# First attention: row tiles in another order, wide rows' softmax sums folded on GpSimd, inverse sums two tiles later

## What is computed

```python
xn = _layernorm(x)
latent_kv = xn @ w_kv_down
k, v = split(latent_kv @ w_kv_up)            # 16 heads x 64
q = xn @ w_q
att = einsum('bqhd,bkhd->bhqk', q, k) * 64 ** -0.5
att = softmax(where(causal, att, -inf))
y = einsum('bhqk,bkhd->bqhd', att, v)
x = x + y @ w_out + ffn(xn)                  # FFN with fp4-rounded inputs and weights
```

## Time and profile before

| | |
|---|---|
| median of 3 runs | 2287.49 us (2284.92 to 2288.25) |
| profiled execution | 2287.97 us |
| its span | 2286.2 us |
| TensorE busy | 2154.7 us, 94% |
| VectorE busy | 1672.4 us, 73% |
| ScalarE busy | 1322.8 us, 58% |
| GpSimd busy | 47.6 us, 2% |
| mean granted TensorE clock | 0.994 |
| one turn, by its first matmul (705.59 to 745.95 us) | 40.36 us |

### The profile page before, as it was taken

How to read it: one execution, slowest core, us unless ns; L and a number is a source line. 1 busy time by engine, 2 the same in 40 slices (tenths; PEclk the granted TensorE clock), 3 DMA queues, 4 the chain that set the end, 5 groups by cost and what they waited for, 6 DMA issues and landing times. The chain is left out here.

```text
span 2286.2 us, 45447 instructions
## 1 busy us (share of the span) xinstructions
PE 2154.7 (94%) x19387; PEld 1343.7 (59%) x19387; DVE 1672.4 (73%) x2210; ACT 1322.8 (58%) x2126; POOL 47.6 (2%) x61
## 2 busy tenths in 40 slices
PE   4999999999999999999999989999999999999998
PEld 2666666676776766767667666544444444444444
DVE  6777777777767777677777775777777777777771
ACT  3655556555565555655556553466666666666666
POOL 5000000000000000000000000100000000000000
PEclk7999999999999999999999999999999999999999
DMA  5000000000000000000000019100001111001000
GB/s 123 1 1 1 1 1 1 1 1 1 1 1 1 1 1 1 1 1 1 1 1 1 1 35 231 48 20 20 20 20 30 27 29 32 20 20 20 11 2 11
DMA packets 41211, 42.60 MB, mean 19 GB/s; under 512 B 21361, under 2 KB 33617, under 8 KB 40882
## 3 DMA queue, kind: packets, MB, share of 16 engines
q1 hardware_dynamic: 39858, 39.05, 7.5%
q10 hardware_dynamic: 1152, 0.64, 0.1%
HBM read 27.71 MB, written 11.70 MB: 17 GB/s over the span
## 5 line engine op out<-in xcount | busy, mean ns | idle before, releaser
L1733 DVE TENSOR_REDUCE nm_half<-slot 128x2 f32<-128x1024 f32 x512 | 606.5, 1222 | 162.8 <-PE slot L1511 118.0
L1714 ACT ACTIVATE pT<-slot 128x1024 f32<-128x1024 f32 x512 | 505.9, 1026 | 270.6 <-PE slot L1620 215.9
L948 ACT ACTIVATE prob<-slot,negmax 128x1024 f32<-128x1024 f32 (+6 forms) x448 | 316.8, 718 | 255.1 <-DVE negmax L1045 181.8
L752 PE MATMUL slot<-k_hl,q_hl 64*128 64x512 f32 (+3 forms) x2560 | 356.1, 359 | 57.7 <-ACT prob L948 54.9
L752 PEld LDWEIGHTS slot<-k_hl,q_hl 64*128 64x128 f32 x2560 | 259.4, 186 | 99.2 <-ACT prob L948 74.3
L790 PEld LDWEIGHTS slot<-ident,prob 128*128 128x128 f32 x2304 | 253.9, 141 | 88.7 <-issue 61.4
L790 PE MATMUL slot<-ident,prob 128*128 128x128 f32 x2304 | 288.6, 275 | 0.9 <-DVE probT L612 0.9
L612 DVE COPY probT<-slot 128x768 f32<-128x768 f32 (+1 forms) x192 | 166.8, 869 | 151.3 <-PE slot L790 148.6
L802 PE MATMUL yspace<-probT,v_sb 128*64 128x512 f32 (+3 forms) x1536 | 276.2, 494 | 0.0
L1586 PE MATMUL yspace<-pT,v 128*32 128x512 f32 x2048 | 266.9, 603 | 1.6 <-ACT y_raw L1701 0.8
L1614 PE MATMUL slot<-qs,ks 49*128 49x512 f32 x1024 | 240.2, 471 | 15.1 <-DVE nm_half L1733 7.5
(11 more groups left out here) (244 smaller groups left out, 2330.3 us busy)
## 6 DMA issues: line engine op xcount, KB each, us to landing
qs<-q_hi SPq DMA_DIRECT2D x64, 64.0 KB
qs<-q_lo SPq DMA_DIRECT2D x64, 64.0 KB
ks<-k_hi SPq DMA_DIRECT2D x64, 64.0 KB
ks<-k_lo SPq DMA_DIRECT2D x64, 64.0 KB
x_tok<-in_L_attn_x_dram SPq DMA_DIRECT2D x4, 512.0 KB, 6.6
q_hi<-qk_out SPq DMA_DIRECT2D x4, 512.0 KB, 4.4
q_lo<-qk_out SPq DMA_DIRECT2D x4, 512.0 KB, 5.3
k_hi<-qk_out SPq DMA_DIRECT2D x4, 512.0 KB, 6.1
```

The costliest lines, as they stand in the source:

```text
L752: nc.tensor.matmul(own_ps[a][:, o:o + m], q_hl[hq][own, i * P:(i + 1) * P], k_hl[hk][own, o:o + m], start=(k == 0), stop=(k == 3 and o + m ...
L948: last = nc.scalar.activation(prob[a][:, p_at(i, 0, w)], ps[:, o:o + w], ACT.Exp, bias=negmax[:, i, a:a + 1], accum_out=sums[:, i, a:a + 1])
L1714: nc.scalar.activation(pT[hp][m % PT_DEEP][:, :, :], slot[at["x", n] % RING][:, :].rearrange("p (j t) -> p j t", t=BANK), ACT.Exp)\
L1733: nc.vector.tensor_reduce(nm_half[:, h, :, p * TPB + i], slot[pos % RING][:, :].rearrange("p (a t) -> p a t", t=BANK), AX.X, ALU.max, nega ...
```

## The change

- `s_list` has the two heads of tile 4 first, then 7, 6, 3 and 5. The items in `yspace` are now (7, 1) and (5, 1). `LONE` is gone: both slots of a pair of items are claimed ahead of its first pass.
- The exponentials of the nine wide items no longer accumulate. GpSimd sums instead: `row_sums(it)` takes both heads of a tile at once, adds the right half of the row to the left half, and does this four times (`FOLDS`), so that 1/16 of the width is left in `parts`. These are 20 additions a turn, each waiting for the one before it. Tiles 0 to 2 still accumulate on ScalarE.
- `invert()` first waits for GpSimd's last fold and reduces `parts` (5 tiles x 2 heads x 64 elements) to `sums`. It now stands behind `next_low` of the keys; before, it stood between the first and second step of the fp4 rounding.
- In the ring, `rsums` moves from before t8 to behind t9, and TensorE and ScalarE do it there. VectorE copies t11 ahead of the first `normalise`.
- ScalarE's first exponential of a turn waits for the folds of the turn before. The ternary rounding comes behind the first turn's folds on GpSimd, and VectorE's wait for it stands one turn later.

```diff
-                prob = [sB(f"prob{a}", [P, P * TPB * (TPB + 1) // 2]) for a in range(2)]
+                prob_all = sB("prob", [P, 2, P * TPB * (TPB + 1) // 2])
+                prob = [prob_all[:, a, :] for a in range(2)]
+                folded = sB("folded", [P, 2, BANK])
+                parts = sB("parts", [P, TPB, 2, HS])
...
-                s_list = [(7, 0), (7, 1), (6, 0), (6, 1), (3, None), (5, 0), (5, 1), (4, 0), (4, 1), (0, None), (1, None), (2, None)]
+                s_list = [(4, 0), (4, 1), (7, 0), (7, 1), (6, 0), (6, 1), (3, None), (5, 0), (5, 1), (0, None), (1, None), (2, None)]
...
-                LONE = {5: 1, 7: 1}
...
+                WIDE = [(1, 4), (3, 7), (5, 6), (6, 3), (8, 5)]
+                FOLDS = 4
...
-                           "t5", "t6", "t7", "rsums", "t8", "t9", "t10", "t11", "hidden", "queries", "down", "out"]
+                           "t5", "t6", "t7", "t8", "t9", "rsums", "t10", "t11", "hidden", "queries", "down", "out"]
...
+                    def row_sums(it):
+
+                        if it:
+                            pool.wait_ge(sums_added, it)
+                        for k, (n, i) in enumerate(WIDE):
+                            score_freed(pool, it, n)
+                            if n and s_list[n][1] is not None:
+                                score_freed(pool, it, n - 1)
+                            w = (i + 1) * P
+                            src = prob_all[:, :, p_at(i, 0, w)]
+                            for f in range(FOLDS):
+                                w //= 2
+                                pool.wait_ge(fold_step, fold_count(it) + k * FOLDS + f)
+                                dst = folded[:, :, 0:w] if f < FOLDS - 1 else parts[:, i, :, 0:w]
+                                nc.gpsimd.tensor_tensor(dst, src[:, :, 0:w], src[:, :, w:2 * w], ALU.add).then_inc(fold_step, 1)
+                                src = folded
...
-                        turned(6)
-                        turned(7)
+                        for m in (6, 7, 8, 9):
+                            turned(m)
                         inverse_sums()
-                        for m in (8, 9, 10):
-                            turned(m)
+                        turned(10)
...
-                                last = nc.scalar.activation(prob[a][:, p_at(i, 0, w)], ps[:, o:o + w], ACT.Exp, bias=negmax[:, i, a:a + 1],
-                                                            accum_out=sums[:, i, a:a + 1])
+                                if n <= C1_LAST:
+                                    last = nc.scalar.activation(prob[a][:, p_at(i, 0, w)], ps[:, o:o + w], ACT.Exp, bias=negmax[:, i, a:a + 1])
+                                else:
...
+                        if it:
+                            act.wait_ge(fold_step, fold_count(it))
...
+                            dve.wait_ge(fold_step, fold_count(it + 1))
+                            nc.vector.tensor_reduce(sums[:, 3:TPB, :], parts[:, 3:TPB, :, :], AX.X, ALU.add).then_inc(sums_added, 1)
+                            dve.wait_ge(sums_added, it + 1)
                             nc.vector.reciprocal(rsum[:, :, :], sums[:, :, :]).then_inc(recip_step, 1)
...
-                        ffn(4, 5)
-                        invert()
-                        ffn(5, 8)
+                        ffn(4, 8)
...
+                        invert()
                         ffn(9, 11)
                         copy_item(7)
                         ffn(11, H_OPS)
                         copy_item(9)

+                        copy_item(11)
+
                         freed(dve, it, TR)
                         dve.wait_ge(pv_done, PV0 + it * NT + C0_FIRST)
                         normalise(1)
-                        copy_item(11)
```

More of the change, by code:

```diff
@@ L482, in two_layers @@
                 t_step = sem("ternary_step")
+                fold_step = sem("fold_step")
+                sums_added = sem("sums_added")
                 moment_step = sem("moment_step")
@@ L632, in normal @@
                             prep_filled(dve, j - 1, 1)
-                        else:
-                            dve.wait_ge(t_step, 10)
                         if j == 2:
@@ L663, in ternary @@
                         nc.gpsimd.tensor_tensor(w, above[:, :], w, ALU.add).then_inc(t_step, 1)
-                    for i in range(2):
-                        ternary(i)
-                    pool.wait_ge(t_step, 10)
+                    nc.gpsimd.memset(parts[:, :, :, :], 0.0).then_inc(fold_step, CLEARS)
+                    def row_sums(it):
[13 more added lines that the diff above has]
+                                src = folded
+                    for it in range(TURNS):
+                        row_sums(it)
+                        if it == 0:
+                            for i in range(2):
+                                ternary(i)
+                            pool.wait_ge(t_step, 10)
                 @blockB.tensor
@@ L757, in scores @@
                                 own_ps = [ps[:, a * BANK:a * BANK + w] for a in range(2)]
[L758 to L764, removed]
                             elif n == 0:
@@ L772, in scores @@
                                 own_ps = [score_claim(n + a)[:, 0:w] for a in range(2)]
-                            for k in passes:
+                            for k in range(4):
                                 one_pass(k, range(2))
@@ L856, in body @@
                         scores(4)
-                        scores(5)
+                        scores(6)
                         scores(7)
@@ L966, in body @@
                         copy_item(6)
+                        copy_item(8)
                         inverse_sums()
-                        copy_item(8)
                         copy_item(10)
@@ L1014, in prep @@
                                 first, last = ((0, 1), (1, 2), (2, 6), (6, 8), (8, 10), (10, PREP_OPS))[2 * (it - turn + 3) + place]
+                                if j == 0 and first == 2:
+                                    dve.wait_ge(t_step, 10)
                                 for k in range(first, last):
```

7 lines of the change are left out of this document (6 added, 1 removed).

## The result

The changed kernel takes 2308.93 us (2306.93 to 2311.75, 4 runs) where the kernel before takes 2287.87 (2284.92 to 2288.60, 4 runs): **ratio 1.0096, 95% interval 1.0081 to 1.0111, slower by 21 us**. The forecast was slower, 2319 us, range 2278 to 2345. The profiled execution has a span of 2305.1 us, 18.9 more than before. The second layer is as it was; all of it is in the 32 turns.

A forecast was written before the change was run, and what follows sets the result against it. TensorE was taken as the bound, its score products idle behind exponentials, with VectorE close behind. Terms -25.7 (score stretch), +22.4 (`rsums`) and +34 (lock) gave +31 on 2287.97: 2319 us, range 2278 to 2345.

The forecast's parts named there:

- the waits ahead of tiles 6 and 5: Sign in the score products: TensorE still waits for exponentials, from +3.5 to +4.05 before tile 6 and 0.95 us before tile 5.
- GpSimd's 19 us a turn: Sign on GpSimd: the folds keep it busy some 19 us in each turn.
- L606 held up: Sign on VectorE: this two-operand step, L594 before the change, takes well over 0.51 us beside a fold.
- t5 waiting for the copy of t3: Sign on TensorE: t5's transposes need their slot at +24.5 and get it at +25.4, after VectorE's copy of t3.
- a turn of 41.3 us: Sign for the whole turn: its length after the change, where the trace before has 40.36 us.
- Score stretch: First score product to `gates`: 1.0 us less in 14 turns, 0.65 in 18 with a preparing step; 25.7 us less.
- `rsums`: TensorE behind t9: waits 0.70 us a turn for slot 2, freed by VectorE's copy of t7; 22.4 us more.
- The folds' own time: GpSimd's additions: 20.6 us a turn, from +4.1 to +24.7; `invert` asks at +27.9, so they alone delay nobody.
- The lock: VectorE steps with operands in SBUF wait for GpSimd's folds, L594 and L598 before t3's copy: 1.07 us a turn, 34 us.
- rival 2: Only VectorE's one-SBUF-operand steps L586, L1871, L1872 are held up, L586 about 0.6 us; 0.5 a turn, 2303 us; chance 0.13.
- Once-only costs: GpSimd's clearing and the ternary steps, done once only: under 1 us.
- The first two terms: Score stretch's 25.7 us less and the wait of `rsums`, 22.4 us more: together -3 us.

The follow-up runs named there:

- orderonly: Kernel before with only the new tile order (4, 7, 6, 3, 5) and no lone passes, sums still on ScalarE: 2278.19 us, ratio 0.9963.
- nofold: Changed kernel without GpSimd's folds and the waits for them, row sums from a constant, reduction kept: 2292.59 us, 1.0031 against the kernel before.
- fold47: Kernel before with the new tile order, GpSimd folding only tiles 4 and 7, reductions and preparing steps where VectorE waits for t1: 2269.86 us, ratio 0.9928.
- c7first: Changed kernel with the copy of t7 right behind the inverse, ahead of two fp4 steps: 2288.57 us, 1.0012 against the kernel before.

## Why the prediction was right, and where not

**The direction, and what makes it, were right:** a gain in the score stretch, as much lost again at `rsums`, and the lock on top. Of its signs, the waits ahead of tiles 6 and 5, the wait of `rsums` and GpSimd's 19 us a turn came; L606 held up, t5 waiting for the copy of t3 and a turn of 41.3 us did not come in a plain turn. There the account is, against before: 0.79 us less to `gates`, 0.11 more from there to t5, 0.06 to t6, 0.89 from t6 to the next `project`, in all 0.27 more.

- *Score stretch*, forecast 25.7 us less. Measured 0.77 to 0.79 in a plain turn and 0.73 in the one shown, some 24 us. Expected were 1.0 and 0.65: the plain turn was overrated, the loss through the preparing steps too (0.35 expected; 0.24 in orderonly). The waits stand ahead of tile 6 (0.55, forecast 0.55) and tile 5 (1.0, forecast 0.95); the one ahead of tile 3 is missing. Not asked was whose gain it is: about three quarters are the order's up to `gates`, 0.39 of 0.71 up to t5.
- *`rsums`*, forecast 0.70 us a turn for slot 2, 22.4 us. The forecast meant a start that is later by 0.70 without what the folds add to it, and that measured 0.73; the 0.70 us of idle time in the changed kernel's row is another quantity, and that it is the same number is chance. 20 us came back when the copy stood first. What the forecast did not see is the cheap mend: the two fp4 steps between.
- *The folds' own time*, forecast 1.8 and 1.0 us for tile 5's first two, and no wait of `invert` for them. Measured 1.89 and 1.16 (the first perhaps with a wait for L606 in it, which is not shown); `invert` never waited.
- *The lock*, forecast 1.07 us a turn, 34 us. **This is the term that was mis-sized.** Measured: 0.22 in a plain turn, and 16 us with the first turn, the last, the table load and the low clock behind them, which nofold took out together. The mechanism is as described, but its phase was off: the forecast had L594 come into the first fold of tile 5, at +21, with L586 among the held steps (0.6 us in rival 2). L586 (L598 of the changed kernel) met the end of a fold and took 0.36 us; L594 (now L606) began at +20.79, the fold at +21.11. With L586 held for 0.6 us it would have come behind the fold's start (an estimate from these numbers). So only L598 was caught. The copy of t3 was 1.2 us late instead of 2.05, and nearly all of that lay in the slack ahead of t5. Where both were caught and the turn has keys, in the middle one, it was 0.7 us from `gates` on, still under the 1.07; in the last turn, without keys, TensorE waited 2.75 us. The rows' conclusion that VectorE's instructions with all operands in SBUF suffer was too wide as well: L602 did not.
- *Once-only costs*, forecast under 1 us. Wrong: the ternary steps meet the fp4 steps in the first turn (4 us against nofold, 1.6 of them in the stretch of low clock), and the wait for the folds moves a table load into the path (1.3 us).

The sum of 31 us was 10 too high. The first two terms gave -3; nofold, which has just these, measured +6, 9 more: the score stretch gained less, and small losses were not in the sum (0.07 us a turn between `gates` and t5, and the turns with late moments). The lock's term was 34 and measured 16, 18 less. That the total came as near as 10 us is in part luck: the two errors have opposite signs.

## What to carry to other kernels

Work given to an idle engine is free only if that engine shares nothing with a busy one: put VectorE's SBUF-to-SBUF steps and GpSimd's instructions at different times, and price the collision by its phase: a shift of under 0.5 us decided here whether one step or two were caught, 0.2 us a turn or 0.7, and 2.2 in the turn without slack behind them. When a change has several parts, try each alone: the order of the tiles was worth 8.5 us and was buried under sums that gave 10 and took 24. Read a delay from start to start, not from the idle time of a row. Put the added step where its engine is idle (fold47), and ahead of a copy that frees a slot put nothing that nobody waits for (c7first).

## What the runs showed of the hardware

- A VectorE TENSOR_TENSOR with both operands in SBUF took 2,027 ns beside a GpSimd addition and 525 beside GpSimd clearing memory; a single-operand TENSOR_SCALAR of 0.18 us took 0.99 beside the clearing. A RECIPROCAL with its operand and its result in SBUF (L602) took 2,352 to 2,355 ns in all 32 turns of the changed kernel, each time beside folds, and 2,352 to 2,356 before.
- The held-up L610, of its own 0.53 us, ends 0.38 us after the GpSimd instruction that it waited for (739.71, 740.09); L1908 and L1909 with one operand, of their own 0.34, end 0.20 us after theirs.
- One more semaphore wait ahead of an exponential put an ACT_TABLE_LOAD of 1.28 us behind the waits instead of ahead of them.
- TensorE's granted clock fell to 1.2 GHz three times in the 32 turns of the changed kernel, each time right after a wait of 1.87 to 2.75 us, and the products behind the wait took up to 1.7 times as long (4.28 us instead of 2.58); without the folds it did not fall.
